# First tiles of experts 0 and 1 from the rows of batches 0 to 13, between the steps of the last batch's routing

## What is computed

```python
x = x + tanh(g_xattn) * attention(layernorm(x), ctx, ctx)     # 16 heads of 16
h = layernorm(x)
bids = sigmoid(h @ conf_w.T + conf_b) * wealth                # 8 experts
top2 = top_k(bids, 2); w = softmax(top2)
x = x + tanh(g_ffn) * sum_e w_e * (silu(h @ gate_e.T) * (h @ up_e.T)) @ down_e.T   # inner 1024
```

## Time and profile before

| | |
|---|---|
| three executions, median | 1198.39 us (1196.59 to 1202.21) |
| the profiled execution | 1202.42 us, span 1200.6 us from first to last instruction |
| busy, share of span | PE 1091.6 us (91%), PEld 75%, DVE 668.0 (56%), ACT 555.3 (46%), POOL 315.6 (26%) |
| mean granted clock of PE | 0.961 |
| attention | 0 to about 500 us |
| first tiles of experts 0 and 1 | 514.73 to 542.40 us |
| expert 2 to the end | 542.40 to 1200.6 us |

### The profile page before, as it was taken

One profiled execution on the slowest core, in us unless ns is written; L12 is line 12 of the kernel. 1 busy time (PEld: TensorE's weight loads), 2 busy tenths in 40 slices (PEclk: granted clock), 3 DMA queues, 4 the chain that ended last, 5 costly groups with the idle time before them and its releaser, 6 DMA issues. The chain is left out here.

```text
span 1200.6 us, 24032 instructions
## 1 busy us (share of the span) xinstructions
PE 1091.6 (91%) x8213; PEld 896.2 (75%) x8213; DVE 668.0 (56%) x1588; ACT 555.3 (46%) x891; POOL 315.6 (26%) x366
## 2 busy tenths in 40 slices
PE   5789999999999988289899999999989999999994
PEld 4456666666666655247599999999849999999994
DVE  2546777777777774365644444444564444444442
ACT  3456676666676664155533333333453333333331
POOL 2122444444343332311311122112221122112111
PEclk8899999999999997589999999999999999999998
DMA  8100111111111101384621121112141122112111
GB/s 297 52 15 24 39 37 44 48 46 37 37 37 37 44 30 48 121 317 164 220 56 32 22 36 32 28 30 36 31 140 28 22 36 36 31 23 36 32 26 23
DMA packets 48025, 72.85 MB, mean 61 GB/s; under 512 B 6256, under 2 KB 42864, under 8 KB 44912
## 3 DMA queue, kind: packets, MB, share of 16 engines
q0 software_dynamic: 16896, 43.53, 14.2%
q1 hardware_dynamic: 30000, 27.68, 7.8%
q10 hardware_dynamic: 1088, 1.11, 0.3%
HBM read 47.14 MB, written 24.90 MB: 60 GB/s over the span
## 5 line engine op out<-in xcount | busy, mean ns | idle before, releaser
L1519 POOL DMA_INDIRECT out<-y,token x64 | 104.6, 1634 | 473.1 <-DVE y L1453 364.1
L1379 ACT ACTIVATE silu<-gate 128x512 f32<-128x512 f32 x128 | 76.5, 597 | 277.4 <-PE up L1287 277.4
L1299 PE MATMUL down<-w_split,h_hi 128*128 128x512 f32 x512 | 185.9, 398 | 0.0
L901 DVE TENSOR_REDUCE max_neg<-maxps 128x4 f32<-128x1024 f32 x128 | 156.4, 1222 | 52.8 <-PE maxps L510 51.1
L1287 PE MATMUL gate<-x_hi,w_split 128*128 128x256 f32 x1024 | 184.5, 282 | 0.0
L1287 PE MATMUL up<-x_hi,w_split 128*128 128x256 f32 x1024 | 183.8, 281 | 0.0
L1444 DVE TENSOR_TENSOR h<-silu,up 128x512 f32<-128x512 f32 x128 | 88.0, 688 | 171.4 <-ACT silu L1379 171.4
L703 ACT ACTIVATE probs<-scores 128x1024 f32<-128x1024 f32 x124 | 127.8, 1030 | 60.5 <-PE scores L535 60.5
L1287 PEld LDWEIGHTS gate<-x_hi,w_split 128*128 128x128 f32 x1024 | 148.8, 188 | 3.0
L1287 PEld LDWEIGHTS up<-x_hi,w_split 128*128 128x128 f32 x1024 | 147.8, 188 | 0.0
L1301 PE MATMUL down<-w_split,h_lo 128*128 128x256 f32 x512 | 144.2, 282 | 0.0
(11 more groups left out here) (164 smaller groups left out, 1756.3 us busy)
## 6 DMA issues: line engine op xcount, KB each, us to landing
xg<-dispatched SPq DMA_DIRECT2D x41, 272.0 KB, 2.8
stage<-gate_T POOLq DMA_DIRECT2D x8, 1024.0 KB, 7.5
stage<-up_T POOLq DMA_DIRECT2D x8, 1024.0 KB, 9.4
stage<-down_T POOLq DMA_DIRECT2D x8, 1024.0 KB, 12.0
x_all<-x SPq DMA_DIRECT2D x16, 256.0 KB, 6.3
ctxT<-ctxT SPq DMA_DIRECT2D x16, 256.0 KB, 2.7
out<-x_all SPq DMA_DIRECT2D x16, 256.0 KB, 2.1
out<-y,token POOLq DMA_INDIRECT x72, 3.8
```

What stands on the lines that cost most here:

```text
L901: V.tensor_reduce(to, maxps[:], AX.X, ALU.max, negate=True).then_inc(s["max_taken"], 1)
L1299: mm(down[t][:].rearrange("p (n d) -> p n d", n=2), h_hi[:, i, rows], split[:, :, cols], start=i == 0, stop=False, skip_group_check=True)
L1379: nc.scalar.activation(silu[pair % 2][:], gate[pair % 2][:], ACT.Silu).then_inc(s_silu, 1)
L1519: pool.indirect_dma_start(out, bass.IndirectOffsetOnAxis(token[:, t:t + 1], axis=0), y[:, t, :], None, compute_op=ALU.add).then_inc(s_adde ...
```

## The change

Experts 0 and 1 (`EARLY = 2`) get their first tiles from the rows that batches 0 to 13 (`KNOWN = 14`) have sent them, loaded before the last two batches are routed.

- Two pad stores at the start, on SP ahead of the context of batch 2, fill the first 128 rows of both experts' regions; POOL waits for them before its loop.
- The weights of expert 1 are loaded by POOL behind the scatter in the body of batch 14, into a buffer of their own; those of expert 2 between the scatters of batches 14 and 15.
- When all rows of batches 0 to 13 are scattered, SP loads 128 rows for each of the two experts.
- A matmul KNOWN on PE sums the counts after batch 13, and DVE raises the running counts of experts 0 and 1 to 128 (`space_early_experts`), so that later rows go behind the first tile.
- PE: turns of both tiles' rows behind `ranks` of batch 14, then expert 0's four products set between `turn_x2`, `logits` and `ranks` of batch 15; then the rest of expert 0 and all of expert 1; then the first rows of expert 2. ACT rounds three parts of expert 0's weights ahead of the norm of batch 15, DVE splits them ahead of its routing. DVE takes the counts behind the first half of h.
- The early tiles use the banks of gate and up for the flips and the down product too. Expert 1's weights are rounded and split only if it has a full tile.
- The pads go to SP (experts 0 to 3) and POOL (4 to 7, behind the last scatter); a SiLU on ACT that only loaded its table is gone.
- Tiles in SBUF are placed in another order, so that the early tiles lie over what is no longer used.

```diff
@@ sync
+            for e in range(EARLY):
+                sp.dma_start(disp[e * REGION:e * REGION + FIRST], pads[:]).then_inc(s["first_rows_padded"], 16)
...
             over_batches(sp, body)
-            store_residual(BATCHES - 1, EPILOGUE)
-            pad_experts(sp, range(0, EXPERTS, 2))
+            sp.wait_ge(s["scattered"], KNOWN * 16 * 2 * QT)
...
+            for e in range(EARLY):
+                sp.dma_start(xg[:, e], disp[e * REGION:e * REGION + FIRST]).then_inc(s_rows, 16)
+            store_last()
+            pad_low()
+            sp.wait_ge(s["pads_stored"], 16)
             attention_over(sp)
+            sp.wait_ge(s_padded[0], 16 * (EXPERTS // 2))
@@ tensor
+            def out_of_last():
+                known_counts()
+                turn_heads(last_batch, 0, EPILOGUE)
+                turn_heads(last_batch, 1, EPILOGUE)
+                turn_normed(EPILOGUE)
+                attn_out(EPILOGUE)
+                EPILOGUE.read(pe, "KNOWN")
+                ranks(last_batch - 1, EPILOGUE)
...
+            out_of_last()
+            pe.wait_ge(s["unit_read"], handed["units"])
+            pe.wait_ge(s["pv_read"], BATCHES * GROUPS)
+            turn_rows(16 * EARLY, EARLY)
+            early_product(0, 0, 0)
+            early_product(0, 0, 1)
+            turn_last_x2()
+            early_product(0, 1, 0)
+            last_logits()
+            early_product(0, 1, 1)
+            ranks_and_counts()
+            early_down(0)
+            early_product(1, 0, 0)
+            early_product(1, 0, 1)
+
+            pe.wait_ge(s_y, TT)
+            early_product(1, 1, 0)
+            early_product(1, 1, 1)
+            early_down(1)
+
+            pe.wait_ge(s_y, EARLY * TT)
+            pe.wait_ge(s_flipped, 2 * EARLY)
+            turn_rows(16 * EARLY + 16)
             over_tiles_hinted(pe, "pe_count", first, rest, before_rest)
@@ scalar
+            out_of_last()
+            act.wait_ge(s_turned, EARLY)
+            nc.scalar.activation(x_early[:], turned[:], ACT.Copy).then_inc(s_xhi, EARLY)
+            for m, half in HALVES[:3]:
+                round_part(0, m, half, s_hi)
+            norm_last()
+            early_silu(0, 0)
+            early_silu(0, 1)
+            read_early_flip(0, 0)
+            round_part(0, *HALVES[3], s_hi)
+            read_early_flip(0, 1)
...
@@ vector
+                V.tensor_scalar(extra[:], known, -1.0, float(FIRST), ALU.mult, ALU.add).then_inc(s["extra_known"], 1)
+                dve.wait_ge(s["extra_known"], 1)
+                V.scalar_tensor_tensor(macc[0:1, 0:EARLY], extra[:], 0.0, macc[0:1, 0:EARLY].bitcast(fp32),
+                                       ALU.max, ALU.add).then_inc(EPILOGUE.freed("KNOWN"), 1)
...
+            rest_of_weights(0, *HALVES[:3])
+            route_last()
+            early_h(0, 0)
+            count()
+            early_h(0, 1)
+            rest_of_weights(0, HALVES[3])
+            dve.wait_ge(s_noted, EARLY)
+            early_y(0)
+            rest_of_weights(0, *HALVES[4:])
+            early_h(1, 0)
+            early_h(1, 1)
+            early_y(1)
             attention_over(dve)
@@ gpsimd
             add_bias(1)
+            pool.wait_ge(s["first_rows_padded"], 16 * EARLY)
...
+                if isinstance(b, int) and b == BATCHES - 2:
+                    for n in range(3):
+                        load_third(pool, 1, n, stage[1])
...
+            pool.wait_ge(s_rows, 16 * EARLY)
+            scatter_next_to_last()
+            pool.wait_ge(s["x2_stored"], 16 * BATCHES)
+            load_weights(EARLY)
+            scatter_last()
...
+            pool.wait_ge(s["pads_stored"], 16)
+            add_early(0, s_added)
+            pool.wait_ge(s_down, 1)
+            for m in range(3):
+                pool.wait_ge(s_split[m], 2)
+            load_weights(EARLY + 1)
+            pool.wait_ge(s_added, 16)
+            add_early(1, s_first_added)
             attention_over(pool)
-            for e in range(1, STAGES):
-                load_weights(e)
```

More of the change, by code:

```diff
@@ L37 @@
 STAGES = 3
+EARLY = 2
+KNOWN = 14
 ROW = 272
@@ L67, in sem @@
             return keep.enter_context(nc.semaphore(name))
-        stage = sb(keep, "stage", [P, WCOLS])
+        stage = [sb(keep, f"stage{i}", [P, WCOLS]) for i in range(EARLY)]
         idn = sb(keep, "idn", [P, P])
@@ new lines, in count @@
+            def count():
+                EPILOGUE2.written(dve, "COUNT")
+                link = chain(dve, "count_chain", 2, 0)
+                link(V.tensor_copy(counts[:], EPILOGUE2.bank("COUNT")[:, 0, 0:EXPERTS]))
+                link(V.tensor_scalar(tiles[:], EPILOGUE2.bank("COUNT")[:, 0, 0:EXPERTS], float(TILE - 1 - FIRST), None, ALU.add))
+                V.tensor_single_scalar(tiles[:], tiles[:], TILE.bit_length() - 1, ALU.arith_shift_right).then_inc(s["counted"], 1)
+            over_batches(dve, body)
@@ L1061, in gpsimd_attention @@
+            return out_of_last, route_last, count
         def gpsimd_attention(pool):
@@ L1186, in expert_stage @@
         s_first_added = sem("first_added")
+        s_own_hi = sem("expert1_weights_hi")
+        s_own_split = [sem(f"expert1_weights_split{n}") for n in range(3)]
         third = WCOLS // 3
@@ L1365, in first, with early_product @@
                 first_contract(e, 1, range(IC // 2)).then_inc(s_down, 1)
-            turn_rows(16)
+            def early_product(e, half, mat):
+                if mat == 0 and half == 0:
+                    pe.wait_ge(s_xhi, EARLY)
+                    for n in range(2):
+                        wait_stage(pe, e, n)
+                for c in range(HC):
+                    last = mm(early_bank((gate, up)[mat], e, half)[:].rearrange("p a b -> p (a b)"),
+                              x_early[:, c, e * FIRST:(e + 1) * FIRST],
+                              weights(stages[e], mat)[:, c, half * (INNER // 2):(half + 1) * (INNER // 2)],
+                              start=c == 0, stop=c == HC - 1)
+                if mat == 1:
+                    last.then_inc(s_pair, 2)
@@ new lines, in early_flip @@
+            def early_flip(e, half):
+                pe.wait_ge(s_made, e * PAIRS + (2 * half + 4))
+                if half == 1:
+                    pe.wait_ge(s_flipped, 2 * e + 1)
+                for i in range(IC // 2):
+                    last = nc.tensor.transpose(early_bank(gate, e, 0)[:].rearrange("p a b -> p (a b)")[:, i * P:(i + 1) * P],
+                                               h[half][:].rearrange("p a b -> p (a b)")[:, i * P:(i + 1) * P], idn[:])
+                last.then_inc(s_flip, 1)
```

362 lines of the change are left out of this document (217 added, 145 removed).

## The result

| | before | after |
|---|---|---|
| median of 20 executions each | 1199.39 us (1195.94 to 1203.96) | 1201.43 us (1199.52 to 1208.48) |
| ratio after to before | | 1.0028, 95% interval 1.0016 to 1.0040 |
| the profiled execution | 1202.42 us, span 1200.6 | 1199.52 us, span 1197.8 |

Forecast were 1185.7 us and a range of 1179 to 1194: a gain of 1.1%. Measured is a loss of 0.3%, small but outside its interval. The two profiled executions stand the other way round (2.9 us in favour of after), because the one of before lies high among its twenty and the one of after lowest among its own. So the traces are used for the lengths of stages, and the ratios for the verdicts.

What follows compares the result with a forecast made beforehand. TensorE bounds the whole; in the changed stretch, experts 0 and 1's first tiles wait for batch 15's routing and rows. 15.7 - 2.0 - 1.0 = 12.7 us off the 1198.39 median gave 1185.7 us, range 1179 to 1194.

Steps and rivals of the forecast that it cites:

- The gap: Between batch 15's routing and expert 2: its first gate matmul starts at 526.7 instead of 542.40, 15.7 us gained.
- the +2.5: Batch 15's routing: z comes at 494.2 instead of 491.65, 2.5 us later, between +1.1 and +7.2.
- this chain is hidden with 2 to 9 us to spare: Batch 15's scatter, pads and load: expert 2's rows land at 514.5 to 521.8, before PE asks at 523.5.
- the tiles don't fill the gap: Rival, 7%: early rows land late or products stall, so expert 0's work starts at 502; gain 7.6 us, 1190.8.
- half clock throughout: Rival, 20%: the products leave PE at 0.50 through batch 15's routing, z is 7.2 us late; 1190.4.
- The case of 1183.1: The new products might leave PE's clock up for the flips at 502, giving back 2.6 us.
- Turn to gate: From turning expert 2's rows to its gate: 2.8 us, plus 0.5 of 0 to 1.1 for skipped tile counts.
- (b): Batch 15's shifts, issued as expert 1's weights are: PE waits 1.0 us more, of 0 to 7.3.
- the rival at 12%: Batch 15's shifts are held behind expert 1's weights and cost the full 7.3 us: 1192.0.
- (a): POOL's wait for two pad stores ahead of batch 2's scale: 2.0 us lost, of 1.5 to 4.
- After 542.40 nothing changes in kind: From expert 2's first gate matmul on, the work stays as before, so only its start time and earlier costs count.
- 5% unnamed: The 5% chance left for what the prediction had not named, with no change in time.

Runs made afterwards that it cites:

- e10: Changed kernel with e3's and e4's edits, and POOL waiting for expert 2's rows before loading expert 3's weights: ratio to before 0.9941.
- e11: e10 with the split weights placed in SBUF ahead of h_hi, x_hi, x_lo and h_lo, as in the kernel before: ratio to before 0.9964.
- e15: e10 with two 128-byte gaps, ahead of the split weights and of h_lo: ratio to before 0.9909, median 1191.21 us.
- e3: Changed kernel with POOL waiting until batch 15's shifts have landed before it issues expert 1's weights: ratio to before 0.9981.
- e16: Changed kernel with only two 128-byte gaps, ahead of the split weights and of h_lo: ratio to before 0.9971, median 1196.68 us.
- e4: Changed kernel with PE's tile counts, branches and full-tile code of experts 0 and 1 left out: ratio to before 0.9980.

## Why the prediction was wrong, step by step

**The gap** (15.7): its size came near, and in this trace its parts too. The products found PE at half clock and the second sped up within (3.78 and 2.80 us), as taken; z came 36.79 us behind the scores of batch 15 for 34.27, which is the +2.5; PE flipped h 0.62 us behind COUNT (taken 0.7); the turn of expert 2's rows came 65.05 us behind the scores for a forecast of 66.1 (523.5 less 457.38), and was held by y and not by rows. But that was luck in part: in seven of the twelve traces the products found full clock, and z came 2 us earlier than before instead of 2.5 later. And "this chain is hidden with 2 to 9 us to spare" failed: in the kernel after, the rows landed at 525.2 (issued at 516.26, 8.9 us under way), 0.5 us ahead of the turn, and in seven of the other eleven traces PE waited for them, 1.5 to 4.2 us, which the prediction itself had named as a sign of being wrong. The rival that the tiles don't fill the gap falls, and so does that of half clock throughout (z 7.2 us late). The case of 1183.1, in which the clock stays up for the flips, didn't come either: the first flip at 504.59 took 1.12 us, for 0.60 before.

**Turn to gate** failed. It was the term "I take 0.5 of 0 to 1.1" on top of 2.8; it measured 6.12, of which 2.65 are left without the branches (e10, e11, e15). The idle of 1.14 us marked issue on DVE was used as a bound for PE; another engine's skip was no row for it. The lost 2.8 us (6.12 less 3.3), set against a turn 1.05 earlier than forecast, are the 1.8 us between 15.7 and 13.9. (The prediction's own sum here, 523.5 and 2.8 and 0.5, is 526.8 and not 526.7.)

**The shifts** were the term (b), 1.0 of 0 to 7.3; they cost 4.7 (3.7 to 4.7 in the seven traces without e3's edit), between that and the 7.3 of the rival at 12%. The reason given for the low end, a row load issued ahead of six weight loads, was of another order: POOL issued the first of the weights at 453.09, SP the shifts at 453.32. The prediction had no row of a small store beside a weight load. The Trainium skill ("DMA: Bandwidth & Descriptors", Queues, rings and completion order), by which the prediction had estimated 2.5 us, pointed the right way and was still 2.2 too low.

**The start wait**, (a), 2.0 of 1.5 to 4, showed in its place and was won back. Counted from the first DVE cast to `max_rows` (44.14, before 45.23), PE's second scores came after 10.0 us for 7.7 before, 2.3 later. What they stood behind last was not the exp but PE's product of the context, whose load SP issues behind the pads: PE waited 0.97 us for it and then did it at half clock (50.44 above); in the kernel before:

```profile
51.01 1.99 PE L463 MATMUL misc<-ctxT,wk_s 128*128 128x256 f32 x8
```

From the first cast to the last one the loop then took 408.7 us, for 409.1 before. Over all traces it took 408.2 to 410.0 in the six kernels with the old order (median 408.8) and 408.7 to 412.1 in the twelve with the new one (409.5). So under 1 us is left of the 2.3 in the usual trace, and "has little room to win it back" was wrong.

**"After 542.40 nothing changes in kind"** failed, with no term and no rival for it, only 5% unnamed. It cost 6.1 us by the distance of buffers (32 tiles of 0.19; e16 gives 6.8 by the ratio) and about 3 by clock: expert 2's first half ran at half clock (3.75 and 3.13 us, where the kernel before has 1.89), behind the hole of 5.47 us. The hole is not shown as the reason: e15 and e11 have none, 1.99 us of idle, and their first product took 3.35 and 3.75 us; in e10, also without, it took 1.96. The two costs are 1.4 more than the 7.8 us by which the stage grew. They came back by chance in the first tiles of experts 3 and 4 (566.70 to 593.90 by the copies of `noted_token`, 27.2 us for 29.1 before; the eighteen traces have 27.0 to 29.4). The change's own line on the order of tiles in SBUF had been read as free.

**The sum.** Forecast 0.9894, measured 1.0028: 16 us. The two traces show 10 of them: 7.8 behind expert 2's gate, 3.7 by the shifts, 1.8 in the gap, less 3.4 at the start (a gain of 1.4 where 2.0 of loss were put). The other 6 lie between traces and medians (the profiled execution of before is 3.0 above its median, that of after 1.9 below its own, and the median of before has since come out 1.0 higher), and no single step is shown for them. e15, which takes shifts, branches, rows and distances back, is 0.9909, so 14 of the 16 us come back with these edits; the interval of e15 holds the forecast. Single ratios don't add exactly: e3 gives 5.6 us, e4 5.8, e16 6.8, but e10 only 10.4 and the gaps on top of it 3.8; each ratio is known to 1.4 to 3.2 us either way. In e10 and e15 part went into the wait for the next rows (4.97 and 4.05 us).

## What to carry to other kernels

Where the diff lays buffers anew, compare a steady tile's period before anything else; the two tiles that a matmul reads from shouldn't start a whole multiple of 1024 bytes apart. A small store that the path waits for is better issued ahead of a large load in another queue; see then for whom the load that is held back comes late. Code stepped over by branches has a price on the engine that takes them, 3 to 6 us here once it was on the path. Where two chains end together, read more than one trace: a clock at its other level in the stage before moved PE by 5 us here and left the end where it was.

## What was not expected of the hardware

- Two operands of a matmul in SBUF at a distance of a multiple of 1024 bytes: 283 to 284 and 401 to 403 ns a matmul instead of 281 to 282 and 398 to 399, 1.1% of a tile that is nothing but matmuls, in all eleven kernels with such a distance; 128 bytes of space take it away. Products with h_lo alone don't show it (281 in after, 282 in before at 720 to 1160). The Trainium skill ("TensorE: Matmul & The Clock Gate", Step-by-step: what each phase is for) says that loading the next weights takes no SBUF bandwidth from the running matmul, since PE has two read ports. What costs the time here isn't shown, a collision of these two ports as little as one with what ACT and DVE write meanwhile; but the time of a matmul does depend on where its operands lie to each other, and the measurement decides.
- Two 8 KB stores issued 0.2 us behind the first of three loads of 1 MB took 7.3 us to be in place for PE (6.3 to 7.3 in seven traces), 2.6 without.
- Two branches over empty experts took PE 3.2 to 3.5 us, some 6 where it had waited for rows just before, and a hint ahead of expert 1's products took only some 2 us off.
- The same instructions found PE at a granted clock of 0.52 to 0.62 in five traces and of 1.00 in seven, from 478 to 492 us. What decides between the two isn't shown.
